# AdaLN block with three-branch attention: skewing the work by tiles instead of by batches

## The chip, the cores and the metric

One core of a Trainium2 chip runs the whole block in float32. Its engines are TensorE (PE in the profile, PEld its weight loads), VectorE (DVE), ScalarE (ACT), GpSimd (POOL) and SyncE (SP), with 16 DMA engines. The metric is the device time of one execution in microseconds (us), lower is better.

## The reference, cut to what matters

x is [8, 1024, 512]: 8 batches of 8 tiles of 128 tokens, 64 tiles in all.

```
mod = silu(c) @ wmod                     # sa, ca, ga, sb, cb, gb per batch
h = layernorm(x) * (1 + ca) + sa
q, k, v = rope(h @ Wq), rope(h @ Wk), h @ Wv         # 16 heads of 32
ck, cv = 64 blocks of 16 tokens, (k + pe) and (v + pe) weighted and summed
out_comp = softmax(q ck^T, blocks wholly in the past) cv
imp = mean over heads and tokens of q ck^T;  top 2 blocks
out_sel = softmax(q k_sel^T, causal) v_sel           # 16 tokens, first 8 of each block
out_win = softmax(q k^T, the last 128 tokens) v
x = x + ga * ((g0 out_comp + g1 out_sel + g2 out_win) @ Wo + bo)   # g = softmax(h @ Wg + bg)
h = layernorm(x) * (1 + cb) + sb
x = x + gb * (h @ base_W^T + base_b + shared + routed(h))   # rank-16 experts, top 2 of 6
```

The choice of the top 2 blocks needs the queries and compressed keys of the whole batch, so selected attention of a batch can't start before its last tile is projected. Window and compressed attention of a tile need only that tile and earlier ones.

## The kernel before, in words

Each engine has one instruction list, written out in advance by small functions called in a fixed order; engines wait on semaphores that count each other's steps. The lists are cut into stages, each a function of the same name on every engine: `head`, `turn`, `first_slot`, `slot`, `end_first`, `end_slot`, `last`.

Before the change the work is skewed by batches. `head` runs seven times and projects tiles 0 to 6 of batch 0 (LayerNorm, transpose, Q, K, V, rotation, transposes of rotated Q and K). `turn` projects a batch's last tile, makes the compressed values of the whole batch (`compress`), importance, choice of blocks, gather, and starts the window attention of tile 0. Then, for seven batches, `first_slot` and six `slot`s each do the attention of tile s of batch b (window, and selected with compressed as one: `cs_scores`, `cs_mask`, `cs_max`, `cs_factor`, `transpose_cs`, `cs_values`), the output and feed-forward of tile s - 1 of batch b (`output`, `residual`, `transpose_h2`, `lora_down`, `router`, `transpose_z`, `feed`, `final`) and the projection of tile s - 1 of batch b + 1. The last batch has no next one: `end_first`, six `end_slot`s and `last` do attention, output and feed-forward alone. The value products of all branches add up in one PSUM tile `ps_o`; `copy_out` takes it to SBUF as `aT`, and `output` multiplies it by Wo.

Selected and compressed scores stand side by side in `ps_s`, 16 + 8(t+1) columns a head for tile t; `ps_s` is written in turn by the compressed scores (L603) and by the window scores of two half groups of heads (L614), and each must be read before the next is written. Two groups of subtraction and normalising are on POOL (L1345, L1353). Probabilities go through PE transposes: the window's in four groups of four heads (L627), the others' likewise (L645), each copied to SBUF by DVE (window, L1658, L1660) or ACT (others, L1127). In every matmul pass of these a head has its own 32 output rows. A float32 matmul is two passes in the records; the projections are split by hand in high and low halves, three passes each (L523 to L525).

Short products share two PSUM banks (`ps_m`), handed round in the order of tables at the top (`SLOT_ORDER` and others); three more banks of `ps_s` serve the heads. `scale_out` and `scale_feed` (POOL, L1361, L1367) multiply the reloaded output and feed-forward weights by the gates of each batch; POOL also adds the bias row to x, raises variances to the power -0.5, adds the two halves of a rotation (L1337), weighs the keys and subtracts the high half of h for the low half.

Of the kernel before, what the change touches and what calls it, by code (L numbers as in the profile page):

```python
# [6 lines left out]
F32 = mybir.dt.float32  # L24
# [9 lines left out]
NT = S // P  # L34
NC = D // P
H, HD = 16, 32
CB, NB = 16, 64
SB, TOPK = 8, 2
NSEL = SB * TOPK
CS = NSEL + NB  # L40
# [5 lines left out]
EPS = 1e-5  # L46


C_ID, C_ROT, C_BLK, C_TOK, C_IO, C_WM, C_CM, C_END = np.cumsum(
    [0, P, NT * 2 * HD, 2 * (NB - 8) + 8, NT * NSEL, 8, 3 * P, NT * NB]).tolist()  # L50

def constants():
# [8 lines left out]
    out[:, C_CM:C_END] = np.where((np.arange(NB) + 1) * CB <= tok, 0, NEG).reshape(P, -1)  # L63
# [6 lines left out]
    out[:, C_BLK:C_TOK] = np.arange(2 * (NB - 8) + 8)[None] - (NB - 8) == p[:, None] // CB  # L70
    out[:, C_TOK:C_IO] = (tok - np.arange(NSEL) % SB).reshape(P, -1)
    out[:, C_IO:C_WM] = np.arange(8)
    return out

# [6 lines left out]
C_UNITS = 3  # L81
GUARD_STEPS = 3 + 6 + 5 + 8 + 1
SETUP_V = GUARD_STEPS + 2
SETUP_G = 6
CS_STEPS = 9
G_STEPS = 3
B_STEPS = 5 + 5 * TOPK
R_STEPS = 13
QUADS = 3 * NT


FIRST_ORDER = [("Q", 0), ("K", 1), ("QT", 0), ("G", 1), ("Y", 0), ("KT", 0),
               ("H2T", 0), ("Z", 1), ("F", 0), ("ZT", 1), ("V", 1), ("HT", 0)]
SLOT_ORDER = [("Y", 1), ("Q", 0), ("K", 1), ("QT", 0), ("G", 0), ("H2T", 0),
              ("Z", 1), ("F", 0), ("KT", 1), ("ZT", 1), ("V", 1), ("HT", 0)]
TURN_ORDER = [("Q", 0), ("Y", 1), ("K", 0), ("QT", 1), ("KT", 0), ("V", 1),
              ("H2T", 0), ("G", 1), ("Z", 0), ("F", 0), ("ZT", 1), ("HT", 1)]
HEAD_ORDER = [("Q", 0), ("K", 1), ("G", 2), ("V", 0), ("HT", 2), ("QT", 1),
              ("KT", 2)]
END_FIRST_ORDER = [("Y", 0), ("H2T", 1), ("Z", 0), ("F", 1), ("ZT", 0)]  # L100
END_SLOT_ORDER = [("Y", 1), ("H2T", 1), ("Z", 0), ("F", 1), ("ZT", 0)]
LAST_ORDER = [("Y", 1), ("H2T", 1), ("Z", 1), ("F", 0), ("ZT", 1)]
C2_UNITS = ("Y", "H2T", "Z", "F", "ZT")


def units_of(orders):

    return [(u, t + (u == "HT"), bank) for t, order in enumerate(orders) for u, bank in order]


SETUP_UNITS = [("MOD0", 0, 0), ("MOD1", 0, 1), ("MODT", 0, 0)]
HEAD_EXTRA = {0: [("MOD2", 0, 4)], 2: [("MOD5", 0, 4)], 4: [("MOD3", 0, 4)], 5: [("MOD4", 0, 4)], 6: [("MODT2", 0, 4)]}

HEAD_UNITS = [("HT", 0, 2)] + [unit for t in range(NT - 1)
                               for unit in [(u, t + (u == "HT"), bank) for u, bank in HEAD_ORDER] + HEAD_EXTRA.get(t, [])]
TURN_UNITS = [(u, NT - 1 + (u == "HT"), bank) for u, bank in TURN_ORDER if u not in C2_UNITS]
SEGMENTS = {"pro": SETUP_UNITS + HEAD_UNITS + TURN_UNITS,
            "loop": units_of([FIRST_ORDER] + [SLOT_ORDER] * (NT - 2) + [TURN_ORDER]),
            "epi": units_of([END_FIRST_ORDER] + [END_SLOT_ORDER] * (NT - 2) + [LAST_ORDER])}


def m_unit(seg, b, name, t):

    i, bank = next((i, u[2]) for i, u in enumerate(SEGMENTS[seg]) if u[:2] == (name, t))
    before = sum(u[2] == bank for u in SEGMENTS[seg][:i])
    per = {s: sum(u[2] == bank for u in units) for s, units in SEGMENTS.items()}
    if seg == "pro":
        return bank, before
    return bank, (b if seg == "loop" else B - 1) * per["loop"] + per["pro"] + before

def quad(t, what):

    order = ("cs", 0, 1) if t > 1 else (0, 1, "cs")
    return 3 * t + order.index(what)
# [12 lines left out]
def blocks_seen(t):  # L149

    return (t + 1) * (P // CB)


def t_spare(t, g):

    return t > 0


def program(nc, x, wqkv, wo, wbt, wa, wb, cT, wmod, bo, bg, rb, wcomp, pe, pet, wg, const, gscr, out):
    with ExitStack() as ctx:  # L160
# [5 lines left out]


# [11 lines left out]
        token = cst[:, C_TOK:C_IO].rearrange("p (t n) -> p t n", t=NT)  # L179
        ident_b = sb("ident_b", [P, P], BF16)  # L180
# [5 lines left out]
        csmask = sb("csmask", [P, NT, CS])  # L186
        wcol = sb("wcol", [P, 1])
        blkw = sb("blkw", [P, C_TOK - C_BLK])
# [3 lines left out]
        ckn = sb("ckn", [P, NC, NB])  # L192
        pe_s = sb("pe_s", [P, D])
        pew = sb("pew", [P, NB])
# [22 lines left out]
        qT = sb("qT", [P, NC, S])  # L217
# [4 lines left out]
        gates = sb("gates", [P, NT, 3])  # L222

        csv = sb("csv", [P, D])

        csk = sb("csk", [P, NC, CS])
# [7 lines left out]
        onehot = sb("onehot", [P, TOPK, NSEL])  # L234
        v_tiles = [ra, rbf]
        tokj = sb("tokj", [P, TOPK, SB])

        css = sb("css", [P, H, CS])
        csp = sb("csp", [P, H, P])
        cm = sb("cm", [P, 2, H])  # L240
        cden = sb("cden", [P, 4, H])
# [4 lines left out]
        pT_prev, pT_own, pT_cs = pT[:, 0], pT[:, 1], pT[:, 2]  # L246
        aT = sb("aT", [P, NC, P])
# [88 lines left out]
        def m_bank(seg, b, name, t):  # L336

            bank, _ = m_unit(seg, b, name, t)
            return ps_m[bank], m_done[bank]
# [1701 lines left out]
```

## Time and profile before

| What | Value |
|---|---|
| median of 3 runs | 2272.89 us (2268.36 to 2275.06) |
| span of the profiled execution | 2265.8 us; its own time isn't recorded beside it |
| PE, DVE, ACT, POOL busy | 2108.9, 1698.7, 1331.8, 792.1 us |
| instructions | 49116 |
| DMA | 89.66 MB, mean 40 GB/s |

A busy share says how long an engine had something in flight, not that it ran at its peak: on PE successive matmuls overlap, so the spacing between them is the cost. The chain of waits tells which engine's work the end depended on. A stretch is read by its length against the busy time of each engine in it.

### The profile page before, as it was taken

The page shows a single profiled execution, that of the slowest core. Times are in us where ns is not written, and L with a number is a line of the kernel's source. Part 1 is how long each engine was busy: PE and PEld are TensorE (multiplying, and loading weights), DVE is VectorE, ACT ScalarE, POOL GpSimd, SP SyncE. Part 2 cuts the span into 40 slices and gives each one's busy share as a digit, 9 for nine tenths or more (in the row PEclk, how much of TensorE's full clock was granted, in tenths as well). Part 3 has the DMA queues.
Part 4 walks back from the last instruction along what each step waited for, and adds up shares of the span by engine and source line. Part 5 has one row for each costly group of instructions (what it writes and reads, how often), then busy time and mean ns, then how long its engine had stood idle before and what let it go on. Part 6 is the DMA issues. An engine that isn't in the chain of part 4 may idle for free.

```text
span 2265.8 us, 49116 instructions
## 1 busy us (share of the span) xinstructions
PE 2108.9 (93%) x17948; PEld 1398.6 (62%) x17948; DVE 1698.7 (75%) x4741; ACT 1331.8 (59%) x4706; POOL 792.1 (35%) x780
## 2 busy tenths in 40 slices
PE   6989999999999999999999999999999999997887
PEld 3656666566665666656665666656666566664454
DVE  4667777777876887777887777777787688776775
ACT  2346666656664665656665665655666566565554
POOL 2433333433334333333343333343333333333121
PEclk9999999999999999999999999999999999998999
DMA  6110000200011000110002000020001100021000
GB/s 219 55 34 25 20 29 29 70 30 29 24 49 55 25 20 30 52 47 29 29 24 75 29 19 26 29 70 29 29 25 52 52 25 20 29 52 38 20 21 19
DMA packets 49022, 89.66 MB, mean 40 GB/s; under 512 B 6888, under 2 KB 6888, under 8 KB 48784
## 3 DMA queue, kind: packets, MB, share of 16 engines
q1 hardware_dynamic: 37520, 68.95, 9.9%
q10 hardware_dynamic: 11264, 17.57, 2.1%
q8 instruction: 145, 2.38, 0.4%
q14 instruction: 93, 0.76, 0.1%
HBM read 69.68 MB, written 16.83 MB: 38 GB/s over the span
## 4 chain that ended last, share of the span: by engine, by line
PE 57%; DVE 26%; ACT 7%; issue 6%; POOL 3%; DMA 1%; SPq 0%; DVEq 0%; POOLq 0%; ACTq 0%
PE ps_m L719 9%; PE ps_o L651 7%; PE ps_m L684 5%; ACT pw L1093 5%; DVE ps_s L1632 4%; PE ps_s L645 4%; PE ps_m L523 4%; PE ps_m L525 4%; PE ps_m L524 4%; PE ps_t L627 4%; DVE wmax L1637 3%; PE ps_m L701 3%; PE ps_s L603 2%; DVE cden L1692 2%; DVE pT L1660 2%
## 5 line engine op out<-in xcount | busy, mean ns | idle before, releaser
L1093 ACT ACTIVATE pw<-ps_s,wmax 128x128 f32<-128x128 f32 x1024 | 359.1, 379 | 241.1 <-DVE wmax L1637 240.1
L523 PE MATMUL ps_m<-w_hi,h_hi 128*128 128x512 f32 x768 | 368.1, 479 | 4.0 <-DVE h_lo L1763 1.4
L1103 ACT ACTIVATE pw<-pw,wden 128x128 f32<-128x128 f32 x1024 | 313.8, 401 | 6.5 <-DVE wden L1647 6.1
L525 PE MATMUL ps_m<-w_hi,h_lo 128*128 128x512 f32 x768 | 303.6, 395 | 0.0
L524 PE MATMUL ps_m<-w_lo,h_hi 128*128 128x512 f32 x768 | 303.6, 395 | 0.0
L684 PE MATMUL ps_m<-wo_s,aT 128*128 128x512 f32 x512 | 259.3, 628 | 6.4 <-ACT v_s L1058 3.7
L719 PE MATMUL ps_m<-wbt_s,h2T 128*128 128x512 f32 x512 | 252.2, 612 | 0.0
L1127 ACT ACTIVATE pT<-ps_s 80x512 f32<-80x512 f32 (+6 forms) x224 | 133.0, 594 | 182.2 <-PE ps_s L645 171.5
L1093 ACT ACTIVATION_READ_ACCUMULATOR pw<-ps_s,wmax 128x1 f32 x1024 | 224.6, 219 | 0.0
L1658 DVE COPY_PREDICATED pT<-keep_prev,ps_t 128x512 f32<-128x512 uint32 x224 | 163.8, 731 | 52.9 <-PE ps_t L627 51.5
L1345 POOL TENSOR_TENSOR css<-css,cm 128x256 f32<-128x256 f32 (+7 forms) x128 | 110.9, 887 | 258.6 <-DVE cm L1684 258.6
L523 PEld LDWEIGHTS ps_m<-w_hi,h_hi 128*128 128x128 f32 x768 | 144.9, 189 | 76.2 <-issue 52.2
L1353 POOL TENSOR_TENSOR csp<-csp,cden 128x256 f32<-128x256 f32 (+7 forms) x128 | 120.5, 961 | 201.9 <-DVE cden L1699 201.9
L1373 POOL TENSOR_TENSOR h_lo<-hT,h_hi 128x512 fp32r<-128x512 f32 x57 | 72.4, 1270 | 334.6 <-ACT h_hi L1053 334.6
L1660 DVE COPY_PREDICATED pT<-keep_own,ps_t 128x512 f32<-128x512 uint32 x256 | 184.4, 720 | 0.3 <-issue 0.3
L651 PE MATMUL ps_o<-pT,v_s 128*32 128x128 f32 x3840 | 166.2, 276 | 10.2 <-DVE pT L1658 5.5
L614 PE MATMUL ps_s<-kT,qT 32*128 32x256 f32 (+1 forms) x2048 | 141.4, 390 | 33.7 <-ACT pw L1093 23.5
L627 PE MATMUL ps_t<-cst,pw 128*128 128x128 f32 x1024 | 162.8, 283 | 9.2 <-ACT pw L1103 6.7
L524 PEld LDWEIGHTS ps_m<-w_lo,h_hi 128*128 128x128 f32 x768 | 145.6, 190 | 39.1 <-issue 21.8
L525 PEld LDWEIGHTS ps_m<-w_hi,h_lo 128*128 128x128 f32 x768 | 144.7, 188 | 35.6
L1671 DVE TENSOR_TENSOR css<-ps_s,csmask 128x256 f32<-128x256 f32 (+7 forms) x128 | 69.7, 586 | 127.8 <-PE ps_s L603 127.8
L1637 DVE TENSOR_REDUCE wmax<-ps_s 128x4 f32<-128x512 f32 x256 | 163.8, 681 | 0.0
(196 smaller groups left out, 4219.5 us busy)
## 6 DMA issues: line engine op xcount, KB each, us to landing
xa<-x_in SPq DMA_DIRECT2D x65, 256.0 KB, 2.9
xc<-x_in SPq DMA_DIRECT2D x64, 256.0 KB, 2.7
out<-t ACTq DMA_DIRECT2D x64, 256.0 KB, 2.1
wo_s<-wo_in SPq DMA_DIRECT2D x8, 1024.0 KB, 9.3
wbt_s<-wbt_in SPq DMA_DIRECT2D x8, 1024.0 KB
gbc<-gate_rows SPq DMA_DIRECT2D x24, 256.0 KB, 5.2
pw<-wmod_in SPq DMA_DIRECT2D x3, 1024.0 KB, 8.0
pT<-wmod_in SPq DMA_DIRECT2D x3, 1024.0 KB, 9.2
```

What stands on the lines that cost most here:

```text
L523: pe_.matmul(ps[:], h_hi[:, c, :], w_hi[:, col, c, :], start=(c == 0), stop=False)
L524: pe_.matmul(ps[:], h_hi[:, c, :], w_lo[:, col, c, :], start=False, stop=False)
L525: mm = pe_.matmul(ps[:], h_lo[:, c, :], w_hi[:, col, c, :], start=False, stop=(c == NC - 1))
L627: mm = pe_.transpose(ps_t[:, j, :], pw[:, head_column(half, j, i), :], ident)
L651: mm = pe_.matmul(ps_o[HD * j:HD * j + HD, c, :], src[0:rows, cols], probs[0:rows, j, :], start=start, stop=stop, skip_group_check=True)
L684: mm = pe_.matmul(ps[:], aT[:, c, :], wo_s[:, c, :], start=(c == 0), stop=(c == NC - 1))
L719: pe_.matmul(ps[:], h2T[:, c, :], wbt_s[:, c, :], start=(c == 0), stop=False)
L1093: ins = act.activation(pw[:, hw, :], ps_w[:, j, i, 1, :], ACT.Exp, bias=wmax[:, hw:hw + 1], accum_out=wden[:, 0, hw:hw + 1])
L1103: act.activation(pw[:, hw, :], pw[:, hw, :], ACT.Copy, scale=wden[:, 2, hw:hw + 1]).then_inc(wn_ok, 1)
L1637: dve.tensor_reduce(wmax[:, h0:h0 + 4].rearrange("p (j i) -> p j i", j=2), ps_w[:, 2 * p:2 * p + 2, :, 1, :], AX.X, ALU.max, negate=True). ...
L1658: dve.copy_predicated(pT_prev[:, g % 2], keep_prev[:].unsqueeze(1).broadcast_to([P, 4, P]), ps_t[:]).then_inc(tw_done, 1)
L1660: dve.copy_predicated(pT_own[:, g % 2], keep_own[:].unsqueeze(1).broadcast_to([P, 4, P]), ps_t[:]).then_inc(tw_done, 1 if t else 2)
```

## The change: what it does

Every stage n from 0 to 72 now does the projection of tile n (of 64, over all batches), window and compressed attention of tile n - 1, selected attention of tile n - 8, and output and feed-forward of tile n - 9. Parts whose tile would lie outside 0 to 63 are left out. `head` runs for n = 0 to 7, `turn` for n = 8, 16, ..., 56, `first_slot` behind each turn, `slot` for the rest, `end_first` for n = 64, `end_slot` for 65 to 71, `last` for 72.

Compressed keys and values are made tile by tile: `sum_keys` writes 8 columns of `ck`; `comp_values` makes 8 rows, `add_blocks` adds the position term, and SP copies these rows inside SBUF to two (tiles 4 to 7) or six places (tiles 0 to 3). The probabilities of several heads now share a transpose (four heads of 32 columns, or two of 64). Selected attention is a branch of its own: full 128-row products against a block-diagonal `kblk` (scores) and `vblk` (values). The window and compressed sum of a tile is written to a DRAM tensor `part` and read back when its selected part is ready; POOL adds the two into `aT`. The queries are kept in a ring of 9 tiles. All units go through two banks with new order tables, and the stages' instruction orders are new on all engines. The last stages' feed weights are scaled in the first `end_slot`. The tables of masks are set up before the first rotation.

```diff
+S_LAG, C_LAG = NT, NT + 1
+SLOTS = TILES + C_LAG
-SLOT_ORDER = [("Y", 1), ("Q", 0), ("K", 1), ("QT", 0), ("G", 0), ("H2T", 0),
-              ("Z", 1), ("F", 0), ("KT", 1), ("ZT", 1), ("V", 1), ("HT", 0)]
+SLOT_ORDER = [("CV", 0), ("Y", 1), ("Q", 0), ("K", 1), ("SS", 0), ("QT", 0), ("G", 0), ("H2T", 0),
+              ("Z", 1), ("F", 0), ("KT", 1), ("ZT", 1), ("ST", 1), ("V", 1), ("SO", 0), ("HT", 0)]
...
             # SP: copies of a tile's compressed values, and the partial output read back
+            def load_part(m):
+                sp.wait_ge(d_po[m % 2], 16 * (m // 2 + 1))
+                if m > 1:
+                    sp.wait_ge(a_ok, m)
+                sp.dma_start(pi[:, m % 2, :], part[m]).then_inc(d_pi[m % 2], 16)
+            def spread_blocks(n):
+                sp.wait_ge(*m_done_at("CV", n))
+                rows = slice(PB * t, PB * t + PB)
+                for k in range(2):
+                    sp.dma_start(cv_two[64 * k:64 * k + 64][rows], cv_new[0:PB, :]).then_inc(d_cv, 16)
+                if t < 4:
+                    for k in range(4):
+                        sp.dma_start(cv_four[32 * k:32 * k + 32][rows], cv_new[0:PB, :]).then_inc(d_cv, 16)
...
             # PE
+            def comp_values(n):
+                pe_.matmul(ps[0:32, :], blkw[:, :], v_s[:, n % NT, :], start=True, stop=True).then_inc(full, 1)
-                for j in range(4):
-                    mm = pe_.transpose(dst[0:rows, j, :], csp[:, NC * j + g, 0:rows], ident)
+                for k in range(4):
+                    mm = pe_.transpose(spare_t[:, k, :], csp[:, P * (4 * r + k):P * (4 * r + k + 1)], ident)
+            def sel_scores(m):
+                for c in range(NC):
+                    mm = pe_.matmul(ps[:, 4 * NSEL * c:4 * NSEL * (c + 1)], qT[:, c, q_at(m)],
+                                    kblk[:, c, :, :].rearrange("p j s -> p (j s)"), start=True, stop=True)
+            def sel_transpose(m):
+                for k in range(2):
+                    mm = pe_.transpose(ps[:, k * P:(k + 1) * P], slp[:, 8 * k:8 * k + 8, :].rearrange("p h s -> p (h s)"), ident)
+            def sel_values(m):
+                for c in range(NC):
+                    mm = pe_.matmul(ps[:, c * P:(c + 1) * P], vblk[:, 4 * c:4 * c + 4, :].rearrange("p h d -> p (h d)"),
+                                    pT_sel[:, c // 2, :], start=True, stop=True)
...
             def slot(n):      # PE
-                cs_scores(b, s)
-                output(seg, b, t, [0])
-                window_scores(b, s, 0)
+                comp_scores(n - 1)
+                comp_values(n - 1)
+                output(n - 9, [0])
+                window_scores(n - 1, 0)
...
+                sel_scores(n - 8)
...
             # ACT: the window and compressed sum leaves for DRAM
-                act.activation(aT[:], ps_o[:], ACT.Copy).then_inc(o_done, 1)
+                act.activation(po[:, w % 2, :], ps_o[:].rearrange("p c n -> p (c n)"), ACT.Copy).then_inc(o_done, 1)
+                act.dma_start(part[w], po[:, w % 2, :]).then_inc(d_po[w % 2], 16)
...
             # POOL
+            def add_part(m):
+                gp.tensor_tensor(aT[:].rearrange("p c n -> p (c n)"), aT[:].rearrange("p c n -> p (c n)"), pi[:, m % 2, :], ALU.add
+                                 ).then_inc(a_ok, 1)
...
             def slot(n):      # DVE, second half
+                window_weights(n - 1, 1)
+                router(n - 9, 0)
+                router(n - 9, 1)
+                sel_factor(n - 8)
+                ln_a(n + 1)
+                final(n - 9)
+                split_probs(n - 1, 2)
+                sum_keys(n)
+                split_probs(n - 1, 3)
+                sum_q(n)
...
             def end_slot(n):  # PE
+                sel_scores(n - 8)
+                output(n - 9, [0, 1, 2, 3])
+                sel_transpose(n - 8)
+                sel_values(n - 8)
+                transpose_h2(n - 9)
+                lora_down(n - 9)
+                feed(n - 9, [0, 1, 2])
+                transpose_z(n - 9)
+                feed(n - 9, [3, NC])
```

## Rows read from the trace of the kernel before

**Rows 1.** The page: busy time (share) by engine, and the chain that ended last.

```profile
PE 2108.9 (93%) x17948; PEld 1398.6 (62%) x17948; DVE 1698.7 (75%) x4741; ACT 1331.8 (59%) x4706; POOL 792.1 (35%) x780
...
PE 57%; DVE 26%; ACT 7%; issue 6%; POOL 3%; DMA 1%; SPq 0%; DVEq 0%; POOLq 0%; ACTq 0%
```

**Rows 2.** Stretches: length, busy us of each engine (count), PE clock, DMA share, GB/s.

```profile
0.00:48.00 48.00, 29.14 (x104) 14.78 (x105) 19.65 (x40) 14.35 (x24) 10.28 (x17) 0.93 0.74 250
48.00:126.50 78.50, 74.40 (x358) 53.45 (x356) 50.38 (x116) 24.78 (x64) 33.78 (x30) 1.00 0.19 59
157.90:2041.20 1883.30, 1803.47 (x15649) 1209.04 (x15645) 1459.77 (x4119) 1156.95 (x4106) 690.96 (x674) 1.00 0.11 35
2041.20:2265.80 224.60, 176.04 (x1644) 105.45 (x1640) 148.41 (x410) 121.37 (x457) 47.07 (x51) 0.90 0.08 24
2081.00:2245.00 164.00, 133.57 (x1337) 81.78 (x1332) 121.35 (x325) 98.80 (x378) 33.99 (x36) 0.93 0.06 19
```

**Rows 3.** Slots of one batch between rotations of Q, same columns.

```profile
1013.80:1045.80 32.00, 31.05 (x283) 21.23 (x279) 25.22 (x73) 20.43 (x74) 10.66 (x11) 1.00 0.08 26
...
1143.10:1176.30 33.20, 31.52 (x287) 21.70 (x287) 26.55 (x73) 20.72 (x74) 12.38 (x11) 1.00 0.07 25
...
sum 268.50, PE 256.76 PEld 172.13 DVE 208.31 ACT 165.03 POOL 98.58; mean PE 32.10 PEld 21.52 DVE 26.04 ACT 20.63 POOL 12.32
```

**Rows 4.** The chain inside two slots: start us, us, what.

```profile
1045.76 0.69 DVE ra L1599
...
1054.56 0.44 PE ps_s L645 x4
1054.99 0.94 PE ps_m L701 x8
1055.93 1.73 PE ps_m L719 x4
...
1067.36 1.50 PE ps_o L651 x48
...
1071.15 1.13 PE ps_s L614 x16
...
1075.05 0.23 PE ps_m L523
...
1101.09 1.09 PE ps_s L603 x32
...
1102.20 1.30 DVE css L1671 x2
```

**Rows 5.** Timeline of a turn: start, us, engine, line, what.

```profile
1213.65 1.89 PE L562 MATMUL ps_s<-v_s,blkw 128*32 128x512 f32 x8
```

**Rows 6.** DVE by form: xcount, busy us, mean ns, idle before.

```profile
L1758 DVE TENSOR_TENSOR t<-ps_m,x 128x512 f32<-128x512 f32 x64 | 43.8, 684 | 22.8 <-PE ps_m L722 22.8
...
L1682 DVE TENSOR_REDUCE cm<-css 128x16 f32<-128x256 f32 x72 | 29.4, 418 | 1.9
...
L1699 DVE TENSOR_SCALAR cden<-cden,gates 128x16 f32<-128x16 f32 x128 | 23.8, 231 | 2.3
...
L1671 DVE TENSOR_TENSOR css<-ps_s,csmask 128x640 f32<-128x640 f32 x16 | 12.4, 819 | 18.5 <-PE ps_s L603 18.5
...
L1671 DVE TENSOR_TENSOR css<-ps_s,csmask 128x192 f32<-128x192 f32 x16 | 5.0, 352 | 9.2 <-PE ps_s L603 9.2
...
L1533 DVE SCALAR_TENSOR_TENSOR x<-x 8x512 f32<-8x512 f32 x2 | 2.3, 1162 | 0.1
```

**Rows 7.** POOL by form, same columns.

```profile
L1337 POOL TENSOR_TENSOR kr<-kr,rbf 128x512 f32<-128x512 f32 x64 | 81.3, 1271 | 109.6 <-DVE rbf L1604 109.6
...
L1367 POOL TENSOR_TENSOR wbt_s<-wbt_s,gbc 128x512 f32<-128x512 f32 x32 | 39.9, 1278 | 1.2 <-DMA wb_s<-wb_in 1.2
```

**Rows 8.** Timeline of the last stage.

```profile
2245.81 3.67 PE L684 MATMUL ps_m<-wo_s,aT 128*128 128x512 f32 x8 [1.03 <-ACT aT L1131]
...
2262.64 0.69 DVE L1758 TENSOR_TENSOR t<-ps_m,x 128x512 f32<-128x512 f32 x1 [2.24 <-PE ps_m L722]
```

More of the change, by code:

```diff
@@ L34 @@
 NT = S // P
+TILES = B * NT
 NC = D // P
@@ L106, in units_of @@
[L106 to L129, printed above, removed]
@@ new lines, in place_units, with blocks_seen, head_width, rounds_of @@
+def place_units():
+    at, count = {}, [0, 0]
+    for name, i, bank in SETUP_UNITS + [(name, index_of(name, n), bank) for n in range(SLOTS) for name, bank in order_of(n)]:
+        if i is not None:
+            at[name, i] = bank, count[bank]
+            count[bank] += 1
+    return at
+UNIT_AT = place_units()
+def blocks_seen(t):
+    return (t + 1) * PB
+def head_width(t):
+    return 32 if t < 4 else 64
+def rounds_of(t):
+    return 1 if t < 4 else 2
+def rounds_before(w):
+    return 12 * (w // NT) + sum(rounds_of(t) for t in range(w % NT))
@@ L139, in group, with values_through, quad @@
+def values_through(k):
+    b, r = divmod(k, 12)
+    t = max(u for u in range(NT) if rounds_before(u) <= r)
+    return 4 * (NT * b + t) + (r - rounds_before(t) + 1) * 4 // rounds_of(t)
+def quad(w, what):
+    return 3 * w + QUADS.index(what)
 def group(g):
@@ new lines, in output @@
+            def output(c, chunks=range(NC)):
+                if not tile(c):
+                    return
+                ps, full = m_target("Y", c)
+                if chunks[0] == 0:
+                    pe_.wait_ge(*m_free_at("Y", c))
+                    pe_.wait_ge(a_ok, c + 2)
+                    if c % NT == 0:
+                        pe_.wait_ge(wo_ok, NC * (c // NT + 1) + 1)
+                for k in chunks:
+                    mm = pe_.matmul(ps[:], aT[:, k, :], wo_s[:, k, :], start=(k == 0), stop=(k == NC - 1))
+                if k == NC - 1:
+                    mm.then_inc(full, 1)
@@ L990, in _ @@
+            transpose_h(0)
+            for n in range(NT):
+                head(n)
+            for b in range(1, B):
+                turn(NT * b)
+                first_slot(NT * b + 1)
+                for n in range(NT * b + 2, NT * b + NT):
+                    slot(n)
+            end_first(TILES)
+            for n in range(TILES + 1, SLOTS - 1):
+                end_slot(n)
+            last(SLOTS - 1)
         @block.scalar
@@ L1306, in _ @@
[L1306 to L1314 removed]
+            for b in range(1, B):
+                turn(NT * b)
+                first_slot(NT * b + 1)
+                for n in range(NT * b + 2, NT * b + NT):
+                    slot(n)
@@ L1317, in _ @@
+            end_first(TILES)
+            for n in range(TILES + 1, SLOTS - 1):
+                end_slot(n)
+            last(SLOTS - 1)
         @block.gpsimd
@@ new lines, in end_slot, with last @@
+            def end_slot(n):
+                sel_mask(n - 8)
+                sel_max(n - 8)
+                sel_factor(n - 8)
+                next_mod_c(n)
+                residual(n - 9)
+                ln_c(n - 9)
+                router(n - 9, 0)
+                router(n - 9, 1)
+                final(n - 9)
+            def last(n):
+                residual(n - 9)
+                ln_c(n - 9)
+                router(n - 9, 0)
+                router(n - 9, 1)
+                final(n - 9)
```

2512 lines of the change are left out of this document (1319 added, 1193 removed).

## The prediction

> **What bounds the kernel now.** Read in this order: the busy line, the chain of waits, the stretches, one batch slot by slot, then the chain inside one slot. The busy line gives PE 93%, DVE 75%, ACT 59%, POOL 35%; the chain that ended last is 57% PE and 26% DVE [rows 1]. Five stretches (four have a row) show where PE isn't full [rows 2]: an opening of 157.9 us (48.0 set-up and first tile, 78.5 for heads with projection alone, 31.4 for the opening's turn), a middle of 1883.3 us in which PE is busy 1803.5, and a closing of 224.6 us in which it is busy 176.0. The middle is 7 rounds of one batch, 269.0 each. Inside a round an ordinary slot lasts 32.0 to 33.2 us, and grows with the tile's place just as DVE's busy time does (25.2 to 26.6), while PE's grows by 0.5 [rows 3]; six such slots take 195.2, so the turn and the first slot together take 73.8.
>
> What PE must do in an ordinary slot I sum by the spacing at which its instructions follow each other in the chain [rows 4], since busy spans overlap: Q, K and V 36 passes of 0.234 = 8.4; output and feed-forward 18 passes of 512 columns at 0.43 = 7.8; twelve groups of four transposes at 0.44 = 5.3, and one of z, 0.1; gate and router products 2 x 0.94 = 1.9; compressed scores 1.1 and window scores 2.2; 92 value passes at 1.50/48 = 2.9. Sum 29.7, so 2.3 to 3.5 us of each slot is PE waiting. Two waits repeat: PE issues compressed scores, then stands until DVE has read them (1.30) before it may write window scores over them; and a run of DVE work behind Q (rotation, window maximum, factors, scaling, first split) ends later than PE's K passes [rows 4]. So the middle is PE's work plus some 9% of waits into which DVE comes.
>
> **PE's work, changed.** Per tile: compressed probabilities go from four groups of transposes to one (tiles 0 to 3) or two (4 to 7), mean 1.5: -2.5 x 0.44 = -1.10. Selected attention becomes its own: scores 8 passes of 128 x 64, values 8 passes of 128 x 128, both priced as the 8 router passes, 0.94 each; two transposes 0.22. The bound for the scores is 0.0 above their spacing and 0.3 below (8 narrow passes at 1.09/32); I take 0.94, the row with full rows and about that width. Compressed values of a tile, 2 passes, cost 1.89/8 each [rows 5], 0.47, in every slot; the 16 such passes and 4 of the position term (0.26 each, like them) leave the turn, -4.8 per batch. The compressed value products stay 32 passes. An ordinary slot thus has 29.7 - 1.10 + 0.94 + 0.94 + 0.22 + 0.47 = 31.2; over a batch the net is +0.87 a tile, 56 us in 64 tiles. Nothing else on PE is dropped: projection, windows, output and feed-forward are the same instructions.
>
> A rule bears on the 32 value passes, now with 8 to 64 rows where they had 72 to 128. Here narrow passes show a floor: 32 compressed-score passes of 32 rows take 1.09, 0.034 each, against 0.031 for value passes of 128 rows [rows 4]. The Trainium skill (TensorEngine Tiling (Array Packing), section Theoretical Speedup) gives up to 2 times for a small dimension of at most 64 and 4 times at most 32. By it the 32 passes would cost a quarter to a half of what they do; by the row they stay.
>
> **DVE's work, changed**, from its forms [rows 6]. Mask: two instructions over 16 + n columns become one over n; by 352 ns for 192 elements and 819 for 640, 1.17 becomes 0.75, -0.42. Maxima and sums of the 16 selected columns (0.42 and 0.41) and their share of the small operations leave, -1.3 in all, and come back for the selected attention: mask 0.42, maximum and sum 0.42 each, four small operations at about 0.2, +2.04. Added: the compressed values (512 columns of PSUM, priced as the final add) 0.68; keys' position term 0.20; per batch 1.1 for spreading keys and values, less 0.86 for the old one. Net +1.2 us a tile, 26.0 to 27.2 of 33. ACT loses 2.5 copies of 0.6 and gains one of 0.6, one of about 0.45 and a DMA issue of 0.34 a tile, about even; it has 12 us free in a slot. POOL gains one 512-column add, 1.27 [rows 7], beside 12 busy now in 32 to 33 [rows 3]; but it stands ahead of the split of h, which Q waits for. Between them and Q lie the compressed scores, compressed values, output and window scores, 6.1 us of PE work, against about 2.5 for the two: covered; without that cover 1.3 a slot.
>
> **DMA and queues.** Each tile's partial output is written to HBM and read back six slots later, 512 KB more per 33 us on engines 11% busy [rows 2]: hidden. SP gets 2 to 6 small copies a tile and the read back, ahead of the input loads. The small copies wait for the compressed values at about 3 us of a slot and are wanted at about 20. If they held SP to the end, the input load for the next tile would come late by some us; it is asked for early in the slot and used at about 24. Taken as 0, bound 0 to 1 us a slot.
>
> **The middle.** In an ordinary slot the wait for the mask is filled: compressed values 0.47 and the first output chunk 0.86 now stand between scores and window scores, and output's input is old and ready. About 0.9 of waiting goes. Behind Q, DVE's run gains the selected mask, maximum and floor (1.0) and loses 0.65 of factors, while PE gets 0.94 of selected scores there: nearly even. In the second half DVE has 16.1 us queued (K's rotation, three splits, weights, router, selected factor, LayerNorm, final, key and query sums) where PE has 15. I take 2.1 of waiting: 31.2 + 2.1 = 33.3, bounds 31.7 (waits 0.5) and 34.6 (DVE 27.2 and its 6.7 to 7 idle of now, with 0.6 of POOL). Turn and first slot: PE -4.8 + 2 x 1.47, DVE +2 x 1.2 + 1.1, and the choice of blocks now stands at the turn's start, where its chain (importance, choice, spread, value load, gather) delays window scores instead of running under K and V. Taken as 73.5, bounds 70 to 80. A round: 6 x 33.3 + 73.5 = 273.3, bounds 260 to 288. Seven rounds 1913; the first turn has no output or feed-forward in it yet, -7: 1906.
>
> **Opening.** A head now carries window and compressed attention of the tile before. PE: 8.4 + gate 0.94 + three transposes 1.32 + 0.47 + 1.09 + 2.2 + four window transposes 1.76 + 0.66 + 2.9 = 19.7. DVE: two rotations 2.9, maxima 5.0, splits 5.8, weights 0.95, LayerNorm 1.6, gates 0.7, sums 1.55, compressed values, mask, maximum and factors 3.7: 22.2. The bound below is DVE's 22.2, above the closing's present slots, 164/6 = 27.3 with DVE busy 20.2 of them [rows 2]. Walking the chain (scores, mask, maximum, rotation, exponentials of half 0, then half 1, splits, key sums, next scores) I get 25.3. Seven: 177. Gate rows in two heads now lie on a filled DVE, eight operations of about 1.16 [rows 6], +9, less 3 for the first windows. Set-up: tables, eleven small fills and casts and one of 2048 columns, about 6 us of DVE by estimate, stand before the first rotation: 48 to 53. Opening 53 + 177 + 6 = 236, against 157.9.
>
> **Closing.** First stage: attention of the last tile, choice of blocks, output; 27.3 + 5.4 of choosing on DVE: 33. Then seven slots with selected attention, output and feed-forward only, which are one serial chain: the present last stage goes from output at 2245.81 to the final add at 2262.64, 16.8 us [rows 8], PE idle for over half. Selected scores ahead of it 0.94, and residual just behind the selected factor: 18.0 each, 126; scaling of the feed weights, five operations of 1.28 on POOL [rows 7], +2; last stage 16.8, store 3.2. 33 + 126 + 2 + 20 = 181, against 224.6.
>
> **Sum.** 236 + 1906 + 181 = 2323 of span, against 2265.8: +78 opening, +23 middle (+30 in the rounds, -7), -44 closing. The execution's own time isn't shown, only its span; the median 2272.9 lies 7.1 above, which I add: 2330.
>
> **Rivals.**
> Waits vanish. With attention's output an old one and one more unit in each gap, PE runs nearly without waits. For it: the mask wait and output's wait go. Against: growth with DVE's time. Slots 31.7, pair 71: round 261, less waiting at the ends (-8): 228 + 7 x 261 - 7 + 181 = 2229, with 7 it is 2236. Faster. Decides: a round under 264.
> DVE becomes the bound: DVE's 1.2 lies wholly on the path with POOL's add, slots 34.4, pair 77, round 283, heads 27: 2323 + 7 x 10 + 12 = 2405, 2412. For it: slots grow as DVE grows [rows 3]. Against it: in the chain PE's instructions follow without a gap for half a slot [rows 4]. The Trainium skill (Perfetto Trace Analysis, section Identifying the Most-Contended Engine) tells one to judge TensorE by LDWEIGHTS busy, here 62%, not matmul busy; by that DVE at 75% is the most contended engine [rows 1]; by the chain it is PE.
> Row groups side by side: value products on four row groups run at once instead of one after the other, so that 32 passes cost a quarter of 1.0 us. For it: they now start at rows 0, 32, 64 and 96. Against: the floor of 0.034 [rows 4]. 2330 - 0.75 x 64 = 2282, just outside no change.
> The skew does nothing (new waits in the middle just eat the shorter closing, heads fill in 22): 2300 or so, inside my range.
>
> **Chances.** Forecast 0.57; waits vanish 0.18; DVE bound 0.18; row groups 0.07. What a measurement can tell from no change is 0.3%, 6.8 us: 2266 to 2280. Faster 0.19, same 0.07, slower 0.74. The likeliest case alone spans 2298 to 2368 (a round 269 to 278). The range takes half of each outer case: 2250 to 2395.
>
> **What would show it.** Opening up to the first turn near 236 with DVE near 22 of 25 in a head; rounds of 273; seven closing slots near 18 each with a clock at times at 1.2 GHz; compressed transposes 384 where they were 1024; PE idle in the middle still 5% or more. It is wrong if a round is under 266, if a head takes under 22, or if the closing slots overlap each other (14 or less).

## The result, and the profile after

The changed kernel takes 2402.9 us (median of 4 runs, 2401.5 to 2405.3) against 2272.1 beside it: ratio 1.0576, 95% interval 1.0562 to 1.0591, slower. The forecast was 2330 us with a range up to 2395. The sign was right and the size was not: +131 us, where +57 was forecast. The profiled execution has a span of 2400.7 us, 134.9 longer than before. Its own time was 2402.5, so that time and span differ by 1.8 us; the forecast had added 7.1 to the span of before, and so the profiled execution of before was probably a quick one.

The page of the changed kernel, busy line and chain, to be held against [rows 1]:

```profile
PE 2263.7 (94%) x18426; PEld 1467.4 (61%) x18426; DVE 1836.3 (76%) x5055; ACT 1303.8 (54%) x4654; POOL 878.4 (37%) x849
...
PE 69%; DVE 18%; issue 6%; POOL 3%; DMA 2%; ACT 2%; SPq 0%; DVEq 0%; POOLq 0%; ACTq 0%
```

The busy shares hardly moved. The chain did: PE's part of it rose from 57% to 69%, DVE's fell from 26% to 18%. PE also has 155 us more of busy time, more than the whole loss.

Opening, middle and closing, cut where the compressed scores of stages 8 and 64 begin (columns as in [rows 2]):

```profile
0.00:239.40 239.40, 202.47 (x1777) 131.53 (x1777) 169.84 (x375) 132.04 (x458) 61.86 (x64) 0.94 0.24 79
239.40:2215.80 1976.40, 1918.93 (x16034) 1256.60 (x16034) 1581.66 (x4367) 1125.09 (x4048) 765.63 (x732) 0.98 0.16 50
2215.80:2400.70 184.90, 142.30 (x627) 79.26 (x623) 84.82 (x313) 46.68 (x149) 50.91 (x53) 0.87 0.16 55
```

| stretch | before | forecast | after |
|---|---|---|---|
| opening | 157.9 | 236 | 239.4 |
| middle | 1883.3 | 1906 | 1976.4 |
| closing | 224.6 | 181 | 184.9 |

So the ends came out within 4 us each, and the middle is 70 us longer than forecast. One round of it, stage by stage (answers [rows 3]): three of its six ordinary slots, then the turn and the first slot:

```profile
912.30:946.30 34.00, 33.66 (x291) 21.94 (x287) 27.43 (x76) 19.80 (x72) 11.68 (x13) 1.00 0.13 43
...
980.40:1014.80 34.40, 34.06 (x295) 22.45 (x291) 28.29 (x76) 20.38 (x73) 12.55 (x13) 1.00 0.12 40
...
1049.30:1083.80 34.50, 33.99 (x299) 22.50 (x295) 28.95 (x78) 19.03 (x70) 12.88 (x12) 1.00 0.12 36
1083.80:1126.50 42.70, 39.04 (x310) 25.32 (x306) 32.70 (x97) 21.77 (x76) 14.71 (x13) 0.92 0.36 105
1126.50:1160.50 34.00, 31.90 (x261) 21.13 (x258) 26.73 (x74) 19.95 (x74) 20.88 (x21) 1.00 0.17 52
```

In an ordinary slot PE is busy in all but 0.3 to 0.5 us of 34; of a slot of before it left 1.0 to 1.7 [rows 3]. The six ordinary slots sum to 205.5 against a forecast of 199.8. At the turn the granted clock is 0.92, the mark of some microseconds at 1.2 GHz. Turn and first slot took 76.7 here and 77.2 to 79.6 in other rounds, 78.0 in the mean, against 73.5.

The chain of waits at the end and the start of a slot shows two products that the forecast had priced too low:

```profile
912.37 1.02 PE ps_s L652 x32
913.39 0.98 PE ps_m L612 x2
914.36 1.05 PE ps_m L784 x2
...
944.20 0.35 PE ps_o L735 x8
944.55 0.57 PE ps_o L698 x16
945.13 0.35 PE ps_o L735 x8
945.48 0.57 PE ps_o L698 x16
```

L612 makes the compressed values of a tile (a pass is one matmul record of PE): two passes take 0.98 us, where the forecast had 0.47 from [rows 5]. L735 and L698 are the compressed and window value products: 24 passes take 0.92 us, 0.038 each, where [rows 4] had 1.50 for 48, 0.031 each.

To see all of PE's work I gave each pass the time to the start of the next, idle time taken out, and took the mean over five ordinary slots of before (1013.8 to 1176.3) and six of after (878.3 to 1083.8), in us a slot:

| PE's work | before | after | change | forecast |
|---|---|---|---|---|
| compressed values (L612) | 0 | 0.98 | +0.98 | +0.47 |
| value products (L651; L698, L735) | 3.25 | 3.91 | +0.66 | 0 |
| selected attention (L747, L770, L758) | 0 | 1.89 | +1.89 | +2.10 |
| transposes of compressed probabilities | 1.79 | 0.81 | -0.98 | -1.10 |
| all else | 26.16 | 26.27 | +0.11 | 0 |
| idle | 1.26 | 0.37 | -0.89 | -0.7 |
| slot | 32.46 | 34.23 | +1.77 | +0.8 |

The forecast of idle time is 2.1 less the 2.8 that its sum left in a slot of before. Two rows hold 1.17 us of an error of 0.97. The experiments ask whether these are real prices, what they are made of, and what the turn adds.

### The profile page after: what moved, and what is told of

The parts are those of the page before. It is cut to its first block, busy times and chain, and to the rows that moved or that the text cites. A ratio compares the mean times of both kernels' runs of the same rounds, so it can differ in the third digit from the quotient of the medians.

```text
span 2400.7 us, 51261 instructions
## 1 busy us (share of the span) xinstructions
PE 2263.7 (94%) x18426; PEld 1467.4 (61%) x18426; DVE 1836.3 (76%) x5055; ACT 1303.8 (54%) x4654; POOL 878.4 (37%) x849
## 4 chain that ended last, share of the span: by engine, by line
PE 69%; DVE 18%; issue 6%; POOL 3%; DMA 2%; ACT 2%; SPq 0%; DVEq 0%; POOLq 0%; ACTq 0%
PE ps_m L784 9%; PE ps_m L830 9%; PE ps_m L582 5%; PE ps_m L583 5%; PE ps_m L584 5%; PE ps_o L698 5%; DVE ps_s L1870 4%; PE ps_s L668 3%; PE ps_t L681 3%; PE ps_o L735 3%; PE ps_m L807 3%; PE ps_s L652 3%; PE ps_m L612 2%; PE ps_m L593 2%; PE ps_m L833 2%
## 5 line engine op out<-in xcount | busy, mean ns | idle before, releaser
L784 PE MATMUL ps_m<-wo_s,aT 128*128 128x512 f32 x512 | 251.3, 618 | 13.5 <-POOL aT L1551 13.5
L830 PE MATMUL ps_m<-wbt_s,h2T 128*128 128x512 f32 x512 | 262.7, 623 | 0.4 <-POOL wb_s L1566 0.4
L1509 POOL TENSOR_TENSOR ra<-ra,rbf 128x512 f32<-128x512 f32 x64 | 83.2, 1300 | 320.0 <-DVE rbf L1841 319.9
L698 PE MATMUL ps_o<-pT,v_s 128*32 128x128 f32 x3840 | 167.5, 281 | 7.1 <-DVE pT L1899 1.3
L784 PEld LDWEIGHTS ps_m<-wo_s,aT 128*128 128x128 f32 x512 | 88.6, 190 | 135.7 <-issue 133.8
L1870 DVE COPY_PREDICATED ps_s<-later,ps_s 128x512 f32<-128x512 uint32 x224 | 144.2, 689 | 33.4 <-PE ps_s L668 33.1
L681 PEld LDWEIGHTS ps_t<-cst,pw 128*128 128x128 f32 x1024 | 121.3, 144 | 59.9 <-issue 36.9
L668 PE MATMUL ps_s<-kT,qT 32*128 32x256 f32 (+1 forms) x2048 | 146.9, 402 | 2.7 <-DVE csp L1911 1.6
L668 PEld LDWEIGHTS ps_s<-kT,qT 32*128 32x128 f32 x2048 | 93.4, 192 | 81.0 <-issue 59.8
```

Of the source, the lines that this page charges most:

```text
L668: mm = pe_.matmul(ps_s[:, j, (i + 1) * 2 * P - n:(i + 1) * 2 * P], qT[rows, c, q_at(w)], kT[rows, c, k0:k0 + n], start=True, stop=True, sk ...
L681: mm = pe_.transpose(ps_t[:, j, :], pw[:, head_column(half, j, i), :], ident)
L698: mm = pe_.matmul(ps_o[HD * j:HD * j + HD, c, :], src[:, cols], probs[:, j, :], start=start, stop=False, skip_group_check=True)
L784: mm = pe_.matmul(ps[:], aT[:, k, :], wo_s[:, k, :], start=(k == 0), stop=(k == NC - 1))
L830: pe_.matmul(ps[:], h2T[:, k, :], wbt_s[:, k, :], start=(k == 0), stop=False)
L1870: dve.copy_predicated(own, later[:].unsqueeze(1).unsqueeze(1).broadcast_to([P, 2, 2, P]), former).then_inc(merged, 1)
```

## The experiments

Theory: PE bounds the middle; its work grew more than forecast, by the two prices and by pauses at the turn. Main rival: DVE's added 1.2 us a tile became the bound (the forecast's rival at 2412 us, the nearest in time to what was measured). Ratios are to the kernel before on the same chip; the changed kernel stands at 1.0576.

### Is it PE or DVE?

**e1_cv_half**, half of the product (`...`: VectorE's addition reads the same half twice):

```diff
-pe_.matmul(ps[0:32, :], blkw[:, :], v_s[:, n % NT, :], start=True, stop=True)
+pe_.matmul(ps[0:32, 0:256], blkw[:, :], v_s[:, n % NT, 0:256], start=True, stop=True)
...
```

> The changed kernel with the product of the compressed values over 256 of their 512 columns alone (the other 256 are left out and filled with the first ones); VectorE's addition keeps its full size. Theory A (TensorE bounds the slot, and the new product costs 0.49 us a pass, 0.98 us a slot): half of it goes, 0.49 us x 64 tiles = 31 us, so 2403 - 31 = 2372 us, ratio to before 1.044; an ordinary slot 33.5 to 34.0 us instead of 34.0 to 34.5. Theory B (VectorE became the bound): nothing on VectorE is shorter, the time stays at 2403 us within 8 (ratio 1.054 to 1.061). Where TensorE's waits give half of it back, 2385 us.

**e2_add_on_act**, which takes an instruction of 0.68 us a tile off DVE:

```diff
-dve.tensor_tensor(cv_new[:], ps[0:32, :], cv_pe[:], ALU.add)
+act.activation(cv_new[:], ps[0:32, :], ACT.Copy)
```

> The changed kernel with VectorE's addition of the compressed values' positions (0.68 us a tile) taken off VectorE: ScalarE copies the product out of the bank at the same place of its own order, and the position term is left out of the compressed values. TensorE's work is the same. Theory A (TensorE bounds): 2403 us, within 8 either way (ratio 1.054 to 1.061). Theory B (VectorE bounds): 0.68 x 64 = 44 us go, 2359 us (ratio 1.038).

Measured: e1 1.0515 (1.0498 to 1.0533), 2393.6 us; e2 1.0577 (1.0551 to 1.0603), 2407.2 us. The slot that lasts from 912.3 to 946.3 in the changed kernel (above, 34.00), in e1 and in e2:

```profile
910.60:944.20 33.60, 33.25 (x291) 21.94 (x287) 27.37 (x76) 19.79 (x72) 11.73 (x13) 1.00 0.14 43
```

```profile
912.10:946.10 34.00, 33.66 (x295) 21.93 (x287) 26.84 (x75) 20.37 (x74) 11.67 (x13) 1.00 0.13 42
```

Taking 0.43 us off PE shortens each ordinary slot by 0.4 to 0.5. In e2 DVE is busy 0.6 us less in this slot, 28 us less in the whole run (1808.5 against 1836.3; not the full 0.68 a tile, since the step that floors the compressed maximum takes 0.36 us where it took 0.24), and the 42 ordinary slots are no shorter (1439.5 against 1438.6 us in all). DVE doesn't bound the ordinary slot. But e1 should have won 31 us and won 14 by the ratios, 8.3 by the profiled spans. In the profiles its 42 ordinary slots together are 18.2 us shorter, and its seven first slots 11.7 us longer. The chain of e1 shows why, in the slot behind a turn:

```profile
1121.00 4.94 POOL wo_s L1559 x4
1125.95 1.23 POOL aT L1551
1127.18 0.09 issue
1127.27 6.43 PE ps_m L784 x8
```

The output product waits for GpSimd, which has to scale the new weights first. In this pause TensorE's clock falls, and eight passes take 6.43 us where the changed kernel has 3.67 in the same round. The granted clock stands at 1.2 GHz from 1126.0 on for 6.8 us. In the last six of the seven rounds, the ones with this pause, it fell at this place each time in e1, for 3.4 or 6.8 us, and once in the changed kernel, where that slot took 36.7 us. A PE that is ready earlier waits longer at that place (2.5 us in the mean of the six, against 1.9), and in e1 it paid again in clock. The length of the pause doesn't decide it alone: the clock fell at pauses of 1.6 and 1.8 us in e1 and stayed up at one of 2.6 in the changed kernel.

### The turn

**e4_two_tiles**: the second half of the gather reads a tile of its own.

```diff
-pe_.matmul(ps[:], onehot[:, j, :], v_tile[:, :], ...)
+pe_.matmul(ps[:], onehot[:, j, :], (v_tile, kr)[j][:, :], ...)
...
-if j:
-    dve.wait_ge(half_sel, b + 2)
-dve.tensor_copy(v_tile[:], v_s[:, at, :].squeeze(1))
+dve.tensor_copy((v_tile, kr)[j][:], v_s[:, at, :].squeeze(1))
```

> The changed kernel with the two halves of the one-hot gather of the selected values each read from a tile of its own (the second from the one that the keys of the last tile stood in), so that VectorE's second copy no longer waits for the first eight passes. Theory A (the wait stands in the turn's only path, TensorE idle 1.1 us at its lower clock, and VectorE's own chain behind it is 2 us shorter): 1 to 3 us in each of 8 turns, 8 to 24 us: 2379 to 2395 us, taken 2387 (ratio 1.0506). Rival (the turn waits for something else, the one-hot products or the load of the blocks): 2403 us within 4.

Measured 1.0493 (1.0475 to 1.0511), 2387.3 us: 19 us. What the edit takes away, in the changed kernel's timeline of a turn (the second copy waits for two passes, not for the eight of the expectation; they run at 1.2 GHz):

```profile
815.02 2.07 PE L634 MATMUL ps_m<-v_tile,onehot 128*128 128x512 f32 x2
817.29 0.43 DVE L2101 COPY v_tile<-v_s 128x512 f32 x1 [2.50 <-PE ps_m L634]
...
818.15 2.08 PE L634 MATMUL ps_m<-v_tile,onehot 128*128 128x512 f32 x2 [1.05 <-DVE onehot L2104]
```

Turns went from 42.7 to 43.7 us down to 40.4 to 41.2, from the second on.

**e5_wo_first**: SyncE asks for the new gates and output weights before the next input tile. The feed weights, other than the expectation says, still come behind it.

```diff
-if n >= NT:
-    load_xc(n - S_LAG + 1)
 if n % NT == 0 and NT < n <= TILES:
...
     load_out()
+if n >= NT:
+    load_xc(n - S_LAG + 1)
+if n % NT == 0 and NT < n <= TILES:
...
     load_feed()
```

> The changed kernel with one thing moved: at a turn, SyncE asks for the gate, output and feed weights of the new batch before it asks for the next input tile, which there waits for the router. Theory (the output product of the slot behind a turn waits 2.3 us for GpSimd's scaling, which waits 3.9 us for these weights; and where that pause drops TensorE's clock to 1.2 GHz the eight output passes take 6.4 instead of 3.7 us): 2.3 us in each of 7 slots and 2.8 in two of them go, 16 to 22 us: 2385 us, ratio to before 1.050 (1.047 to 1.053). Rival (GpSimd is then held by the selected factors ahead of the scaling, and the output product waits as before): 2403 us within 4, ratio 1.056 to 1.060.

Measured 1.0482 (1.0465 to 1.0500), 2386.2 us: 21 us. PE's wait for the scaled sum, whole run, in the changed kernel and in e5 (us in total, times, longest):

```profile
PE ps_m L784 <- POOL aT L1551: 13.5, 7, 2.6
```

```profile
PE ps_m L785 <- POOL aT L1552: 1.3, 1, 1.3
```

The six first slots with the pause fell to 32.4 or 32.5 us from 33.7 to 36.7 (that of the first round had no pause and took 32.4 already), and the eight output passes behind a turn take 3.70 us, at 2.4 GHz. In two rounds the clock fell one slot later instead, and that slot took 35.7 for 34.1; no run shows why.

### The price of the compressed values

In before, [rows 5] has 1.89 us for eight passes. They went to two column groups, that is, two sets of 32 output rows. Either a pass costs 0.236 us, or it costs 0.43 and two groups work side by side.

**e3_before_serial** and **e11_one_strip**, both on the kernel before (in e3 the wait for the last tile's V, left out here, also moves, to the second group):

```diff
-for t in tiles:
-    for k in range(2):            # column group
+for k in range(2):                # e3
+    for t in tiles:
...
```

```diff
-    for k in range(2):
+    for k in range(1):            # e11
```

> The kernel before with one change: the sixteen passes that make a round's compressed values are issued with the group of output columns in the outer loop and the tile in the inner one, so that no two passes in a row go to different column groups; each pass and each sum is the same. The row of before has 1.89 us for eight such passes, 0.236 each. Theory A (two passes that follow each other in different column groups run side by side, and a pass by itself costs 0.49 us as in the changed kernel): 16 x 0.25 = 4.1 us a round, 8 rounds, 33 us: 2272 + 33 = 2305 us (ratio 1.014); if VectorE hides half of it, 2289 us. Rival (a pass costs 0.236 us wherever it stands, and 0.49 in the changed kernel is something else): 2272 us within 4.

> The kernel before with the products of the compressed values for one of the two column groups alone (the other half of the compressed values is left out but for its position term): 8 passes a round instead of 16. Theory A (the two column groups run side by side, each at 0.43 us a pass, whatever order they are issued in): those that are left stand at 0.43 us apart, nothing is won: 2275 us within 4. Rival (a pass costs 0.236 us): 8 x 0.236 = 1.9 us a round, 15 us in 8 rounds, 2260 us, ratio 0.993.

Measured: e3 0.9982 (0.9973 to 0.9992), 2272.0 us, no loss and if anything a little faster; e11 1.0002 (0.9992 to 1.0011), 2276.3 us. The passes in e3 and then in e11 (start, us, engine, line):

```profile
945.93 1.91 PE L562 MATMUL ps_s<-v_s,blkw 128*32 128x512 f32 x8
```

```profile
948.85 1.88 PE L562 MATMUL ps_s<-v_s,blkw 128*32 128x512 f32 x4
```

Four passes in one group take what eight in two groups take. So a pass costs 0.43 us of its group's time, and the two groups run at the same time. e3 missed: I had expected the pairs to need alternate issue. Eight passes issued group by group still ran in pairs, starting 7 to 30 ns apart, so four queued passes of one group don't hold up the other. The Trainium skill (TensorEngine Tiling (Array Packing), section Key Properties) says that tiles operate independently; the runs agree.

**e6_cv_pair** uses this in the changed kernel:

```diff
-pe_.matmul(ps[0:32, :], blkw, v_s[:, n % NT, :], ...)
+for k in range(2):
+    pe_.matmul(ps[32 * k:32 * k + 32, 0:256], blkw, v_s[:, n % NT, 256 * k:256 * k + 256], ...)
...
```

> The changed kernel with a tile's compressed values as two products of 256 columns, one in each of two column groups of 32, where it had one of 512 columns in one group; VectorE's addition runs over 64 partitions of 256 elements, and the copies to the replicas are 4 or 12 a tile instead of 2 or 6. Nothing is left out. Theory A (products in different column groups run side by side): the passes cost 0.55 us a slot instead of 0.98, and VectorE's addition 0.35 instead of 0.68; TensorE bounds the slot, so 0.43 x 55 slots = 24 us go where nothing gives it back, and 9 to 14 us as in the halved product where the pause at a turn costs TensorE its clock: 2379 to 2394 us, taken 2390 (ratio 1.0515). Rival (they follow each other like any two passes): 4 passes of 0.24 = 0.98 us, 2403 us within 4. If the added small copies on SyncE delay the inputs: slower than 2403.

Measured 1.0506 (1.0476 to 1.0535), 2387.1 us. Its chain has four passes in the place of 0.98 for two:

```profile
902.43 0.56 PE ps_m L617 x4
```

Ordinary slots are 33.6 to 34.1 us. Like e1 it gave part back behind the turns.

### The price of the value products

**e7_full_rows** runs the 32 compressed value passes over all 128 rows; **e8_group_cs** keeps them and issues them together:

```diff
-mm = pe_.matmul(ps_o[...], src[at:at + n, cols], pT_cs[at:at + n, k % 2, block_, :], ...)
+mm = pe_.matmul(ps_o[...], v_s[:, t, cols], pT_cs[:, k % 2, block_, :], ...)      # e7
```

```diff
-cs_values(n - 1, 1)
 window_values(n - 1, 2)
-cs_values(n - 1, 2)
 window_values(n - 1, 3)
+cs_values(n - 1, 1)                                                            # e8
+cs_values(n - 1, 2)
 cs_values(n - 1, 3)
```

> The changed kernel with the 32 passes of the compressed value products over all 128 rows, on V's own tile, in place of the 8 to 64 rows of compressed values (the compressed attention's result is left out, what comes out is a sum of other values). The number of passes and all else stay. Theory (each change between passes over a part of the rows and passes over all rows costs 0.1 us, eight changes a tile): 96 value passes cost 3.1 us a slot instead of 3.9, 0.7 x 64 = 45 us at most, and some given back at the turns: 2365 to 2380 us, ratio 1.042 to 1.047. Rival (a narrow pass costs as much as a full one, and the dearer spacing of 38 ns has another reason, the split into short runs): 2403 us within 4. The forecast's rival 'row groups side by side' would have full passes slower: 2403 + 0.75 x 64 = 2450 us.

> The changed kernel with the value products reordered at the end of a slot: window values of groups 2 and 3 first, then the compressed ones of groups 1, 2 and 3 in a row (before: alternating), and window values 1 ahead of compressed values 0. Nothing is left out. Theory (a change between partial and full rows costs 0.1 us): four of eight changes a tile go, 0.4 us a slot, 26 us at most, some of it given back at the turns: 2380 to 2392 us, ratio 1.047 to 1.053. Rival (order of shapes costs nothing): 2403 us within 4; if window group 3 isn't ready a microsecond earlier, TensorE waits for VectorE and the time rises to 2410 or so.

Measured: e7 1.0438 (1.0419 to 1.0456), 2374.7 us; e8 1.0517 (1.0499 to 1.0534), 2392.3 us. The chain of e7, same kind of passes as above:

```profile
1028.48 0.22 PE ps_o L735 x8
1028.70 0.44 PE ps_o L698 x16
1029.13 0.22 PE ps_o L735 x8
```

24 passes take 0.66 us instead of 0.92: two changes of shape cost 0.26. The start times of the passes in the trace put the cost at the change itself: from the last pass of one group to the first of the next it is 0.20 us in the changed kernel and 0.09 in e7, in every ordinary slot. They also show why the rival "row groups side by side" could gain nothing. The four heads of a group have their own output rows, and their passes start 7 ns apart, four by four every 0.11 us, with 24 rows as with 128: they ran side by side already. In e8 the ordinary slot is 0.4 us shorter for half of the changes:

```profile
906.00:939.60 33.60, 33.25 (x295) 22.11 (x291) 27.46 (x76) 19.64 (x74) 11.70 (x13) 1.00 0.14 43
```

The Trainium skill (TensorEngine Tiling (Array Packing), section Key Properties) says that switching the tiling mode drains TensorE. The runs agree, at 0.10 to 0.13 us for each change of shape here. The prediction weighed another section of that page and missed this one.

### Do they add up?

**e9_three** has the edits of e4, e5 and e6; **e10_four** adds that of e8. Their diffs are those above.

> The changed kernel with three of the edits tried singly: the weights of a turn asked for first, the gather's two halves from two tiles, compressed values in two column groups. Nothing is left out. Singly they gave, as ratios to before, 1.0482, 1.0493 and 1.0506 where the changed kernel has 1.0576: 0.0094, 0.0083 and 0.0070. If they are independent they add up to 0.0247: ratio 1.033, 2349 us by a before of 2274. If each had its gain cut by TensorE's lower clock at the turns, which the first removes, the sum is larger: the third has 0.45 us in each of 55 slots, 25 us, where alone it gave 16: ratio 1.029, 2340 us. Rival (the slots are held by VectorE once TensorE is shorter): ratio 1.04.

> As the one before, with the value products reordered as well (window values 2 and 3 first, compressed values 1 to 3 in a row behind them). Theory (TensorE's own work bounds the slot, a change of shape costs 0.1 us): another 0.41 us in each of 55 slots, 22 us, ratio 1.019 to 1.023, 2318 to 2326 us; an ordinary slot 33.2 to 33.7 us. Rival (VectorE's 28 us of work with its waits now ends last): no more than 8 us below the kernel with three edits, ratio 1.026 or more.

Measured: e9 1.0325 (1.0308 to 1.0343), 2349.1 us, the plain sum (1.0329). e10 1.0249 (1.0231 to 1.0266), 2331.9 us; the fourth edit gave 17 us where 22 were expected. The 22 counted 55 slots. In the profiles the 42 ordinary ones gave all of it (1427.3 us in e9, 1409.5 in e10); the seven first slots gave 0.1 and the seven turns 1.4, and the closing took 1.7 back. A slot of e10:

```profile
642.50:675.70 33.20, 32.86 (x293) 22.15 (x289) 27.50 (x76) 19.76 (x73) 12.14 (x13) 1.00 0.13 44
```

PE's idle time in it is still 0.3 us: PE goes on being the bound. It is some 74 us faster than the changed kernel (0.0327 of 2276). The kernel before stays the fastest.

### What bounds the kernel before?

The changed order puts the gate products behind K's third group; before has a wait of 0.69 us ahead of them in 42 slots (us in total, times, longest):

```profile
PE ps_m L544 <- ACT qT L1063: 28.8, 42, 0.7
```

**e12_before_gates** moves them in the kernel before:

```diff
-gate_logits(seg, b, t, [0, 1, 2, 3])
-project(seg, b, t, "K", 1, [2, 3])
+project(seg, b, t, "K", 1, [2])
+gate_logits(seg, b, t, [0, 1, 2, 3])
+project(seg, b, t, "K", 1, [3])
```

> The kernel before with one piece of the changed one's order: in an ordinary slot the third K group is issued ahead of the gate products and only the fourth behind them. Nothing is left out. In the trace of before TensorE waits 0.69 us for qT ahead of the gate products in each of 42 slots, 28.8 us in all. Theory A (TensorE bounds the slot there): the 0.70 us of K fill the wait, 20 to 29 us go, ratio 0.987 to 0.991. Rival (the run of VectorE's work behind Q ends later than K's passes in any case, so the wait turns up again ahead of the window values or the next transposes): less than 8 us, ratio 0.997 to 1.001.

Measured 1.0027 (1.0017 to 1.0037): no gain, slightly slower. Ordinary slots kept their length to 0.1 us, but for three of the 42. The wait for qT is gone, and these have grown by 28.1 us in its place (the first had 5.5 us before, the second 4.3, the third isn't among the waits of before):

```profile
PE ps_o L651 <- DVE pT L1659: 15.0, 42, 0.7
...
PE ps_m L693 <- DVE xc L1570: 11.6, 9, 3.2
PE ps_m L693 <- DVE gl L1621: 11.3, 35, 0.6
```

So in the slots of before DVE's run behind Q sets the pace of that half, although PE is busy 96% of the time. The changed kernel has filled those waits, and each 0.1 us of PE's work counts in full. The three longer slots took 1.3 or 1.4 us more, each with a stretch of 3.4 us at 1.2 GHz that before doesn't have there: 4 us of the profiled execution. Whether they are the whole of the small loss isn't shown.

## Why the prediction was wrong

**Opening, +78 forecast, +81.5 measured.** Right in size, and only in part for its reason. The forecast took heads of 25.3 us from a chain of DVE's work and put PE at 19.7. One head, 134.7 to 159.9:

```profile
134.70:159.90 25.20, 25.20 (x251) 16.25 (x250) 20.85 (x46) 16.86 (x62) 7.79 (x8) 1.00 0.09 26
```

PE has no idle time in it, nor in the head before. The forecast left out a modulation product that the first four of the seven heads carry, and the prices above:

```profile
146.82 3.53 PE ps_m L529 x8
```

19.7 + 3.53 + 0.51 + about 0.7 gives 24.4 of 25.2. The last three heads have no such product and still take 26.2 to 26.9 us, with PE idle for 1.9 to 3.2 of them at a granted clock of 0.93 or 0.94. One of them, and the longest of PE's waits from 134 us on:

```profile
186.20:213.20 27.00, 23.94 (x247) 16.96 (x246) 21.46 (x47) 17.06 (x62) 8.66 (x8) 0.94 0.07 22
```

```profile
PE ps_t L681 <- DVE pT L1901: 6.7, 3, 2.4
```

There PE waits for DVE, as the forecast had it for all seven.

**Closing, -44 forecast, -39.7 measured.** End slots took 17.2 us each against 18.0, with PE at times at 1.2 GHz, as said; the serial chain was read rightly from [rows 8]. The stages before them, 2215.8 to 2276.7, took the rest.

```profile
2276.70:2293.90 17.20, 13.83 (x51) 7.59 (x50) 7.17 (x30) 3.84 (x11) 4.27 (x5) 0.90 0.14 46
```

**The middle, +23 forecast, +93 measured.** The step that failed is the sum of PE's work in an ordinary slot, 31.2 + 2.1 waits = 33.3, measured 34.2 (33.9 of work, 0.4 idle). Two of its terms were mis-sized:
- "Compressed values of a tile, 2 passes, cost 1.89/8 each": 0.47 forecast, 0.98 measured. The row has eight passes of which two always ran together (e11); a lone product has its second pass 0.45 us after its first, and the next product, of another shape, starts 0.52 after that.
- "The compressed value products stay 32 passes", priced at no change: +0.66 measured. Their number stayed, but passes over a part of the rows now stand between passes over all rows, which the kernel before, with 72 to 128 rows, did not have (e7, e8).

The other terms held: selected attention 1.89 against 2.10, transposes -0.98 against -1.10 (384 passes where there were 1024, as forecast). Real waiting in a slot fell by 0.89 us, 0.7 forecast; the "2.1 of waiting" that the forecast kept was mostly work that its sum of chain pieces had missed, 29.7 where the passes take 31.2 in before. These two errors nearly cancel, and that is luck. Six slots give 205.5 - 199.8 = 5.7 us a round.

Turn and first slot were 73.5 forecast and 78.0 measured. 2.3 of the 4.5 is the same two prices, twice. Two pauses stand in these stages, and the forecast named neither: GpSimd's scaling, late because SyncE's queue holds the weights behind an input load that waits for the router (e5), and one tile for both halves of the gather (e4). "Taken as 0, bound 0 to 1 us a slot" for SyncE's queue looked at the small copies and at the wrong load. Clock is lost with them: from the second turn on the changed kernel spends 6.8 or 10.2 us of a turn at 1.2 GHz, e4 3.4 or 6.8. But the seven turns of e4 are 16.7 us shorter and the seven first slots of e5 13.5, 4.3 us a round in all, where only 2.2 of the 4.5 are left to explain; so the forecast's 73.5 was some 2 us too high in something else, which no run here shows.

Six rounds of 5.7 + 4.5 and 9.0 in the first (275.3 against 266.3) are the 70 us. With the four edits of e10 the middle is 1908 us, and the forecast had 1906; the errors above that cancel are still in that 1906, so the agreement is partly chance.

**Rivals.** "DVE becomes the bound" named 2412 us and is nearest in number, but false: e2 took 28 us of busy time off DVE, and the time stayed. "Waits vanish" had its mechanism right, and PE's added work ate it. "Row groups side by side" had the wrong sign: the passes were side by side by output rows already, and the narrow ones brought changes of shape. The doubt on PE's busy share led to DVE at 75%, and the ordinary slot turned out to be all PE.

What is open: 0.11 us a slot of other PE work, some 2 us in the forecast's turn and first slot, when a pause costs clock and when it doesn't, and how much of the small loss in e12 is clock.

## What to carry to other kernels

Price a pass from a row in which it stands alone, as it will in the new place: a group of narrow passes may have run two or four at a time, and its mean is then too low. Count how often neighbouring passes differ in rows or columns used, and put equal shapes next to each other. Where the bound engine must pause for a load once a round, look at the order of the load queue first, since every microsecond saved elsewhere turns into a longer pause there and may cost clock.

## What the runs showed of the hardware

- Two products on different groups of 32 output rows run side by side: eight passes of 512 columns took 1.89 us, four in one group 1.88, also where all of one group's passes are issued first.
- A change between value passes over 8 to 64 rows and value passes over all 128 costs 0.10 to 0.13 us, in this kernel 0.7 us a slot (e7, e8). Between changes, passes of four heads start 7 ns apart and the next four 0.11 us later, whether over 24 rows or 128.
- In e1 TensorE's granted clock stood at 1.2 GHz for 6.8 us around a pause of 2.7 us ahead of the output product, at a cost of 2.8 us. In the changed kernel pauses of 1.2 to 2.6 us at the same place passed at 2.4 GHz in five of six rounds, while in e1 pauses of 1.6 and 1.8 us did not: the length of the pause alone doesn't tell.
